# Linear attention and gated MLP on one core: the value block moved from odd to even slots, the rows' transposes from even to odd

## The reference

```
x = x + layernorm(attention(layernorm(x)))
x = x + layernorm(ffn(layernorm(x)))

attention: q = rope(x Wq^T), k = rope(x Wk^T), v = x Wv^T      16 query heads, 4 key/value heads, 128 each
           qf = elu(q) + 1,  kf = elu(k) + 1
           state += kf v^T,  z += kf   (causal, over the sequence)
           out = (qf state) / (qf z + eps),  then out Wo^T
ffn:       h = silu(x Wg) * (x Wu),  of every 4 neighbours of h the 2 largest in size are kept,  then h Wd
```

## Time and profile before

| | |
|---|---|
| runs | 1225.1, 1226.01, 1226.18 us (median 1226.01) |
| profiled execution, span from first to last instruction | 1224.5 us |
| what lies around the span (median less span) | 1.5 us |
| PE busy | 1198.1 us, 98% |
| DVE, ACT, POOL busy | 741.2, 550.4, 497.9 us (61, 45, 41%) |
| attention slots 0 to 63 | from 40.5 to about 681 us |

### The profile page before, as it was taken

One profiled execution on the slowest core, in us unless ns is written; L12 is line 12 of the kernel. 1 busy time (PEld: TensorE's weight loads), 2 busy tenths in 40 slices (PEclk: granted clock), 3 DMA queues, 4 the chain that ended last, 5 costly groups with the idle time before them and its releaser, 6 DMA issues. The chain is left out here.

```text
span 1224.5 us, 16075 instructions
## 1 busy us (share of the span) xinstructions
PE 1198.1 (98%) x6014; PEld 1006.0 (82%) x6014; DVE 741.2 (61%) x1272; ACT 550.4 (45%) x1061; POOL 497.9 (41%) x403
## 2 busy tenths in 40 slices
PE   8899999999999999999998999999999999999997
PEld 7788888888888788888887878888888878888876
DVE  8656564645575556556564366677556655566568
ACT  5554555545545545455545433332323332333332
POOL 5433442514455425243235444342434653333415
PEclk9999999999999999999999999999999999999999
DMA  7231322222334223222133322121113321111211
GB/s 232 74 86 37 85 69 52 78 52 70 89 92 121 69 61 87 65 76 68 35 80 111 112 60 82 38 70 35 53 52 104 112 78 43 53 52 43 60 44 69
DMA packets 50349, 90.31 MB, mean 74 GB/s; under 512 B 6496, under 2 KB 6752, under 8 KB 50272
## 3 DMA queue, kind: packets, MB, share of 16 engines
q1 hardware_dynamic: 50272, 89.29, 25.8%
HBM read 64.09 MB, written 8.39 MB: 59 GB/s over the span
## 5 line engine op out<-in xcount | busy, mean ns | idle before, releaser
L1244 POOL TENSOR_TENSOR w_lo<-stage,w_hi 128x512 fp32r<-128x512 f32 x96 | 129.6, 1364 | 258.9 <-ACT w_hi L802 258.1
L510 PE MATMUL bank_q<-x_hi,w_hi 128*128 128x512 f32 x436 | 175.2, 402 | 1.3 <-DVE scratch L1025 1.3
L512 PE MATMUL bank_q<-x_lo,w_hi 128*128 128x512 f32 x436 | 171.3, 393 | 0.0
L511 PE MATMUL bank_q<-x_hi,w_lo 128*128 128x512 f32 x436 | 170.7, 392 | 0.0
L1244 POOL TENSOR_TENSOR big_lo<-hidden,big_hi 128x512 fp32r<-128x512 f32 x30 | 69.0, 2319 | 192.8 <-ACT big_hi L922 192.8
L913 ACT ACTIVATE scratch<-hidden 128x512 f32<-128x512 f32 x64 | 40.6, 634 | 206.9 <-DVE hidden L1165 206.9
L1244 POOL TENSOR_TENSOR big_lo<-q_rows,big_hi 128x1024 fp32r<-128x1024 f32 x31 | 76.3, 2460 | 77.4 <-ACT big_hi L844 77.2
L1062 DVE TENSOR_SCALAR small<-bank_od 128x4 f32<-128x4 f32 x61 | 9.7, 159 | 153.5 <-PE bank_od L636 97.5
L511 PE MATMUL bank_y<-wout_hi,a_lo 128*128 128x512 f32 x256 | 100.6, 393 | 0.0
L512 PE MATMUL bank_y<-wout_lo,a_hi 128*128 128x512 f32 x256 | 100.6, 393 | 0.0
L510 PE MATMUL bank_y<-wout_hi,a_hi 128*128 128x512 f32 x256 | 100.5, 393 | 0.0
(11 more groups left out here) (333 smaller groups left out, 3022.4 us busy)
## 6 DMA issues: line engine op xcount, KB each, us to landing
q_rows<-scratch SPq DMA_DIRECT2D x124, 128.0 KB, 2.3
x_rows<-x SPq DMA_DIRECT2D x48, 256.0 KB, 3.0
stage<-wq SPq DMA_DIRECT2D x32, 256.0 KB, 2.8
stage<-wo SPq DMA_DIRECT2D x32, 256.0 KB, 2.7
stage<-wg SPq DMA_DIRECT2D x32, 256.0 KB, 2.7
stage<-wu SPq DMA_DIRECT2D x32, 256.0 KB, 2.8
stage<-wd SPq DMA_DIRECT2D x32, 256.0 KB, 2.7
x<-x_rows SPq DMA_DIRECT2D x16, 256.0 KB, 2.6
```

The lines of the kernel that those rows point to most:

```text
L510: pe.matmul(ps, whi, xhi, start=first, stop=False, skip_group_check=True)
L511: pe.matmul(ps, wlo, xhi, start=False, stop=False, skip_group_check=True)
L512: return pe.matmul(ps, whi, xlo, start=False, stop=last, skip_group_check=True)
L1244: return pool.tensor_tensor(dst, full, hi.bitcast(F32), ALU.subtract)
```

## The change

The value block goes one slot later, from slots 4p-3 to 4p-2. Row transposes go to odd slots only: those of slots 6, 10, 14, 18 go to 5, 9, 13, 17, and those of 42, 46, 50, 54 to 41, 45, 49, 53; the others stay. A transpose in a slot 4p-3 waits for the first operation of `rotate_keys` (which frees bank_t) in place of the copy of the values, and the value block waits for the low parts of the rows turned so far. The statistics of a block of rows go from the end of VectorE's slot, two slots ahead of the transpose, to behind `rotate_sum`, one slot ahead. No instruction is added or removed.

```diff
@@ -56,7 +56,7 @@
 
 
 def v_slot(p):
-    return 4 * p - 3
+    return 4 * p - 2
 
 
 
@@ -65,8 +65,8 @@
 TURNS = [j for j in JOBS if j[0] in ("in", "mid")]
 ADDS = [j for j in JOBS if j[0] in ("res", "out")]
 ROWS = JOBS[TT:-TT]
-IN_1 = [3, 6, 7, 10, 11, 14, 15, 18]
-MID_0 = [39, 42, 43, 46, 47, 50, 51, 54]
+IN_1 = [3, 5, 7, 9, 11, 13, 15, 17]
+MID_0 = [39, 41, 43, 45, 47, 49, 51, 53]
 MID_1 = [8, 10, 12, 14, 16, 18, 20, 22]
 
 
@@ -564,6 +564,7 @@
                 split_wait(g, ("v", p // 2, 0))
                 if p:
                     g.wait_ge(dve_k1, p + 1)
+                    g.wait_ge(dve_xl, turned[0])
                 project(value_bank(p)[:, :], 5, p // 8 * 2 + p % 2).then_inc(pe_v, 1)
 
             turned = [0]
@@ -678,9 +679,9 @@
                 if 1 <= p < STEPS and s == v_slot(p):
                     values(p)
 
-                if s % 4 != 3:
+                if s % 4 == 1:
                     for job in jobs:
-                        g.wait_ge(act_vt, s // 4 + 2)
+                        g.wait_ge(dve_k1, s // 4 + 2)
                         turn(job)
                         turned[0] += 1
 
@@ -1074,6 +1075,8 @@
                                       ALU.mult).then_inc(dve_s, 1)
                 if s % 2 == 0 and 0 < s and s + 4 < 2 * STEPS * 2:
                     rotate_sum((s + 4) // 2)
+                for job in at(tick, norm_tick, [j for j in TURNS if j in LATER]):
+                    variance(job)
                 for p in range(1, STEPS):
                     if s == k_slot(p) + 1:
                         rotate_keys(p)
@@ -1105,7 +1108,7 @@
                 if s % 4 == 3:
                     for job in at(tick, lambda j: turn_tick(*j), [j for j in TURNS if j in LATER]):
                         split_x(job)
-                for job in at(tick, stat_tick, LATER):
+                for job in at(tick, stat_tick, [j for j in ADDS if j in LATER]):
                     variance(job)
 
             def pair(i, c, steps):
```

## The result

The changed kernel takes 1231.68 us (median of 4 runs, 1230.95 to 1232.52), the kernel before, on the same chip, 1225.55 us (4 runs, 1224.43 to 1226.18). The ratio is 1.0052, with a 95% interval of 1.0038 to 1.0067: 6.1 us or 0.5% slower. The forecast was 1232.6.

The account below looks back on a forecast made before the run. PE was taken as the bound, busy 1198.1 of 1224.5 us, so only waits and clock could move the time. Eight unit terms sum to +6.6 us: span 1231.1, plus 1.5 for the median, 1232.6; range 1229.5 to 1236.5.

Parts of the forecast that it names:

- K(8u+2): Start of the key-query product of slot 8u+2, forecast 7.04 us after slot 8u+1's; new PE wait 1.1 us.
- T(8u+2): Start of the transposes of quotients in slot 8u+2, forecast 11.40 us after slot 8u+1's key-query product starts; second wait 0.84.
- T(8u+3): Start of the transposes of quotients in slot 8u+3, forecast 22.78 us after slot 8u+1's key-query product starts.
- The waits of T(11), T(43) and T(51): PE's waits at the transposes of quotients in slots 11, 43 and 51, forecast to be gone.
- Slots 8u+5: Value block out of these seven slots: forecast 0 us, PE staying later than VectorE's chain.
- The eight units: Windows from slot 8u+1's key-query product to slot 8u+3's transposes of quotients; changes forecast for each, summing to +6.6 us.
- the 1.7 us that slot 60 lost: Slot 60, part run at 1.2 GHz before: loss forecast to stay; the sum is 1.7 us less if it goes.
- the low part waits for VectorE's own list: In slot 8u+1 VectorE's low part of the quotients ends at 6.97 us and holds the next key-query product.
- 1: Rival: VectorE's L1044 in slot 17 loses its stretch, 1.61 to 0.74 us; +1.3 us, 1227.3; chance 0.08.
- 2: Rival: short slot 8u+1 costs nothing, VectorE reaching slot 8u+2's reciprocal 1.97 us earlier; 1217 us; chance 0.04.
- 3: Rival: PE's clock falls at the new pairs of waits, 1.7 us each; 1244.6, or 1238.5 for half; chance 0.08.
- 4: Rival: value block waits for the rows' low parts, 0.5 us in three slots; 1234.1; counted within the forecast's 0.80.

Follow-up runs that it names:

- move_5: Changed kernel, but only the value blocks of slots 8u+5 move one slot later, with their row transposes; statistics in even slots: 1223.47 us, ratio 0.9979 to the kernel before.
- move_1: Changed kernel, but only the value blocks of slots 8u+1 move one slot later; statistics in even slots: 1230.92 us, ratio 1.0046 to the kernel before.
- even_stats: Kernel before with only the statistics of row blocks moved to the even one of the two slots ahead of their transpose: 1222.23 us, ratio 0.9973.
- even_stats_33: even_stats with the statistics of the row sum in slot 33 also moved, to slot 34: 1222.54 us, ratio 0.9974 to the kernel before.
- narrow_1: Changed kernel with VectorE's query sum in slots 8u+1 done on 4 columns of one head, not 128x1024: 1232.14 us, ratio 1.0054 to the kernel before.
- pool_behind: Changed kernel with GpSimd's low parts of the third and fourth Wo block in slots 8u+1 held until VectorE's L1045 is done: 1240.65 us, ratio 1.0126.
- stats_back: Changed kernel with the statistics of the row blocks back at their old place, two slots ahead of the transpose: 1235.12 us, ratio 1.0086 to the kernel before.

## Why the prediction was right, point by point

- **Place and mechanism.** K(8u+2) at 7.04 was forecast, 7.03 came (7.11 in unit 33, 8.15 in unit 1, whose slot starts late); T(8u+2) at 11.40 (12.48 in unit 1, 12.52 in unit 33), came at 11.40 to 11.42 (12.54, 12.55); T(8u+3) at 22.78, came at 22.80 to 22.84 in units 9, 17, 25, 41 and 49. The waits of T(11), T(43) and T(51) are gone, as forecast. Slots 8u+5 at nothing: shown by move_5 and move_1.
- **The eight units.** Every term of the sum came within 0.1 us (units 25 and 33 are taken up to the product behind T(8u+3), the others up to T(8u+3)):

  | unit | 1 | 9 | 17 | 25 | 33 | 41 | 49 | 57 |
  |---|---|---|---|---|---|---|---|---|
  | forecast | +1.46 | -0.26 | +1.54 | +1.64 | +0.06 | +0.90 | +0.72 | +0.58 |
  | measured | +1.56 | -0.24 | +1.59 | +1.67 | +0.11 | +0.95 | +0.75 | +0.51 |

  The first seven were forecast at 6.06 together, and K(1) to K(57) is 6.04 longer. That the two agree to 0.02 is chance: the seven measured terms are 6.39, and 0.35 of that came back behind the windows. Of unit 57's +0.51 only 0.12 was left at K(60), since the wait ahead of it went from 2.03 to 1.65.
- **PE's clock, and some luck.** The sum kept the 1.7 us that slot 60 lost; of the two bounds named this was the wrong one. Slot 60 took 6.32 us at 1.00, against 7.91 at 0.78 before, so the tail from K(57) is 1.46 shorter and not 0.58 longer. From K(1) to K(62) the change cost 4.6 us, where the sum has 6.6. In the profiled executions a start 1.2 us later covered most of the difference, and that is luck. At the new pairs of waits the clock did not fall: 1.00 in all eight windows. Why it stayed up in slot 60 is not shown. PE was busy 3.11 of the 4.76 us before slot 60, and 3.11 of 5.14 before; but even_stats has the kernel before's two waits there (1.69 and 2.02 us, before 1.67 and 2.03) and kept its clock all the same, while move_5 and even_stats_33 with these waits lost it:

```profile
650.23:656.55 6.32, 6.32 (x41) 1.00 0.42 128
```

- **One reason was incomplete.** The forecast said that the low part waits for VectorE's own list. That list, and ScalarE's key terms and copy, are two chains of the same length, so the number came out right without the second. narrow_1 showed that shortening the one alone brings nothing. Likewise T(8u+2) had the mask close behind the quotients.
- **Rivals.** 1: the stretch stayed, 1.61; pool_behind shows that it follows GpSimd's work, and that the one other place tried for this work was worse. 2: the short slot did cost; what it put forward in its favour, the statistics, was worth 4.1 us and is in the sum. 3: no fall of the clock in the changed kernel, whose waits there are 1.0 us or less (1.7 in slot 34); behind waits of 2.2, in pool_behind, it fell in two slots. 4: the value block waited nowhere in slots 8u+2.

The trace gave the terms of the eight units to 0.1 us. What it could not give, the clock of slot 60 and the scatter of the start, is what most of the range's width was for.

## What to carry to other kernels

When work is moved between two stretches of an engine that is busy throughout, write down for both stretches what the other engines need in them; a stretch that loses more work than the others' chains leave room for gives the rest back as a wait, and the stretch that gains pays in full. Before shortening the operation that a wait names, look for a second chain of the same length that ends at the same place: only shortening both showed anything here. And separate the parts of a change: the small one (statistics out of the tight slots) was worth 0.3% by itself, while the block moves around it cost it and more.

## What was not expected of the hardware

- VectorE's operations with all inputs in SBUF took 0.9 to 1.1 us more in slot 17 when they began while a low part ran on GpSimd (0.74 to 1.61, 0.69 to 1.81, 1.22 to 2.29), while those with an input in a PSUM bank did not change beside GpSimd's work (in the changed kernel 0.68 for L1044 and 1.22 for L1022 in slots 17 and 18). The Trainium skill (GPSIMD Engine Reference, 1. Specifications) names such a contention of two SBUF inputs with GpSimd; the trace agrees and puts this size on it. In the changed kernel L1045 of slot 17 ended at 222.24, 0.54 us after the last of GpSimd's four low parts. Not every overlap costs: in slot 15 of the changed kernel L1036 began at 197.15, 0.66 us ahead of a low part on GpSimd, and took its 1.22 us.
- The time from the start to K(1), with the same instructions in all kernels, fell between 46.45 and 51.62 us in 14 profiles. Part of this is the granted clock, whose mean up to K(1) was 1.00 in three profiles (K(1) at 46.45 to 47.71), 0.96 or 0.97 in ten, and 0.90 in stats_back, the one with 51.62. For differences of a few us a stretch between two marks inside the program tells more than the whole time.
